# Couples' loop and the expert steps behind it: norm and routing one tanh later, Silu's table first, the softmax's exponential second

## The reference

```python
x = x + jnp.tanh(g_xattn[2]) * _L2_xattn_ref(_layernorm(x), mask, ctx, ...)
#   tanh(x@W + ctx@Ws + b) @ w over all couples (row f, text s) of a batch; softmax over s (masked);
#   tanh of the weighted sums u, v gives a scale and a shift of the normed row
x = x + jnp.tanh(g_ffn[2]) * _L2_ffn_ref(_layernorm(x), ...)
def _L2_ffn_ref(x, ...):
    weights, indices = _gate(x2, Wg)           # sigmoid, 2 of 4 groups, 4 of 16 experts
    for e in range(E):                          # E = 16, hidden 128
        we = jnp.sum(weights * (indices == e), axis=-1)
        h = jax.nn.silu(x2 @ W1[e].T + b1[e]) * (x2 @ W3[e].T + b3[e])
        y = y + (h @ W2[e].T + b2[e]) * we[:, None]
```

## Time and profile before

| | us |
|---|---|
| median of 3 runs | 599.48 (597.36 to 603.2) |
| the profiled execution | 601.89 |
| its span, first to last instruction | 600.1 |
| couples' loop, first to last sum on TensorE | 283.2 to 352.2 |
| expert steps 0 to 15 on TensorE (`up`) | 346.1 to 390.7 |

### The profile page before, as it was taken

One profiled execution on the slowest core, in us unless ns is written; L12 is line 12 of the kernel. 1 busy time (PEld: TensorE's weight loads), 2 busy tenths in 40 slices (PEclk: granted clock), 3 DMA queues, 4 the chain that ended last, 5 costly groups with the idle time before them and its releaser, 6 DMA issues.

```text
span 600.1 us, 8818 instructions
## 1 busy us (share of the span) xinstructions
PE 566.8 (94%) x3305; PEld 394.1 (66%) x3310; DVE 447.4 (75%) x696; ACT 415.2 (69%) x579; POOL 103.8 (17%) x69
## 2 busy tenths in 40 slices
PE   7999999989999999999896989999998999999997
PEld 5688787656677777775230436566545777888886
DVE  4378987588657898987989676766766847787786
ACT  4798999756755556647999765534513858888885
POOL 5400000001200000003989703200000210000000
PEclk9999999999999999999999799999998999999999
DMA  6207210200200811020000024505510110812100
GB/s 237 71 12 307 71 35 2 74 2 2 76 0 4 317 55 58 2 70 1 5 1 1 1 71 120 164 2 153 163 35 2 37 37 0 301 52 72 37 0 35
DMA packets 16782, 40.27 MB, mean 67 GB/s; under 512 B 1834, under 2 KB 6058, under 8 KB 16740
## 3 DMA queue, kind: packets, MB, share of 16 engines
q1 hardware_dynamic: 16740, 39.71, 19.9%
HBM read 39.01 MB, written 0.70 MB: 66 GB/s over the span
## 4 chain that ended last, share of the span: by engine, by line
PE 71%; DVE 14%; ACT 10%; issue 3%; POOL 1%; DVEq 0%; ACTq 0%; POOLq 0%
PE ps L713 38%; ACT work L1094 6%; PE ps L756 4%; PE ps L452 3%; DVE h_lo L1609 2%; PE ps L469 2%; PE ps L739 2%; PE ps L584 2%; PE ps L741 2%; PE ps L555 2%; PE ps L740 2%; PE ps L569 2%; PE ps L459 2%; PE ps L695 2%; DVE h_act L1586 1%
## 5 line engine op out<-in xcount | busy, mean ns | idle before, releaser
L1609 DVE TENSOR_TENSOR h_lo<-h_act,h_hi 128x512 fp32r<-128x512 f32 (+1 forms) x136 | 118.4, 874 | 39.8 <-ACT h_hi L1139 39.0
L713 PE MATMUL ps<-n_hi,w_hi 128*128 128x512 f32 (+1 forms) x232 | 85.4, 402 | 2.0 <-DVE h_act L1586 1.3
L1139 ACT CAST h_hi<-h_act 128x1024 fp32r<-128x1024 f32 (+1 forms) x88 | 75.3, 856 | 14.6 <-PE ps L713 12.1
L713 PE MATMUL ps<-n_hi,w_lo 128*128 128x512 f32 (+1 forms) x232 | 83.0, 391 | 0.0
L713 PE MATMUL ps<-n_lo,w_hi 128*128 128x512 f32 (+1 forms) x232 | 83.0, 391 | 0.0
L1817 POOL TENSOR_TENSOR rstd<-var_eps,minus_half 128x4 f32<-128x4 f32 x16 | 17.5, 1093 | 319.4 <-DVE var_eps L1273 319.4
L713 PE MATMUL ps<-h_hi,w_hi 128*128 128x512 f32 (+1 forms) x184 | 65.5, 398 | 0.1
L713 PE MATMUL ps<-h_hi,w_lo 128*128 128x512 f32 (+1 forms) x184 | 64.0, 390 | 0.0
L713 PE MATMUL ps<-h_lo,w_hi 128*128 128x512 f32 (+1 forms) x184 | 63.9, 389 | 0.0
L1094 ACT ACTIVATE work<-work,p_rest 128x2048 f32<-128x2048 f32 x31 | 59.5, 1998 | 0.4 <-DVE work L1468 0.4
L1132 ACT ACTIVATE h_act<-ps 128x512 f32<-128x512 f32 (+1 forms) x48 | 28.6, 596 | 40.4 <-PE ps L713 40.4
(11 more groups left out here) (234 smaller groups left out, 1023.7 us busy)
## 6 DMA issues: line engine op xcount, KB each, us to landing
work<-g_rows SPq DMA_DIRECT2D x36, 512.0 KB, 6.4
w_f<-in_w SPq DMA_DIRECT2D x20, 512.0 KB, 3.6
w_f<-in_w SPq DMA_DIRECT2D x8, 544.0 KB, 3.6
work<-in_w SPq DMA_DIRECT2D x2, 512.0 KB, 4.3
work<-g_rows SPq DMA_DIRECT2D x4, 256.0 KB, 9.7
p_rest<-in_p_rest SPq DMA_DIRECT2D x1, 714.0 KB, 9.8
p_attn<-in_p_attn SPq DMA_DIRECT2D x1, 546.5 KB, 6.9
x<-in_xT SPq DMA_DIRECT2D x1, 512.0 KB, 3.6
```

The costliest lines, as they stand in the source:

```text
L713: mm = pe.matmul(dst[i], wap(wt, e, lo, size, rows), mv[i], start=(first and c == 0), stop=(last and c == 2))
L1139: act.copy(places(h_hi, m, step), places(h_act, m, step)).then_inc(s["hi"], 1)
L1609: dve.tensor_tensor(lo, src, hi.bitcast(F32), ALU.subtract).then_inc(s["lo"], 1)
```

## The change

On TensorE `up(0)` and `up(1)` move one round later, ahead of the sums of rounds 30 and 31; 4 fillers stand in place of 14; steps 3 to 13 stand closer together around the bias, the weights' matmuls, the norm and the gates. On ScalarE all four first high halves come before the loop's first tanh; square and copy of norm 5 stand ahead of round 27, its high half and the first routing ahead of round 30. Behind the loop Silu's table and the Silu of steps 0 and 1 come first, then the gates' copy, the exponential's table, the softmax's exponential, and Silu's table again. `load_table` writes a column of its own each time. VectorE does products 0 and 1 ahead of the softmax, one between the halves of the weighing, and is one to three products further on at each place behind; its scratch tile `t3` is another. On GpSimd the power of norm 5, half 1, stands behind expert 10.

```diff
@@ -218,7 +218,7 @@
         pairs = work[:, 0:12 * T].rearrange("p (r c) -> p r c", r=6)
         g_all = work[:, 4 * T:12 * T].rearrange("p (e t) -> p e t", e=8)
         g_half = work[:, 4 * T:12 * T].rearrange("p (e t) -> p e t", e=16)
-        table = sb("table", [P, 1])
+        table = sb("table", [P, 16])
         h_part = [h_act[:, i // 2, (i % 2) * HALF:(i % 2 + 1) * HALF] for i in range(4)]
         h_part += [y_g[:, i // 2, (i % 2) * HALF:(i % 2 + 1) * HALF] for i in range(4)]
         values1 = vblk[0][:].rearrange("p b h c -> p (b h c)")
@@ -794,35 +794,35 @@
 
                 if L == 2:
                     for g in pair_sums():
-                        if g == 29:
+                        if g == 30:
                             pe.wait_ge(ln["lo"], 2 * L + 1)
                             up(0)
-                        if g == 30:
+                        if g == 31:
                             pe.wait_ge(x2["sumA"], own_sums(2 * B - 1))
                             up(1)
                     turn_gates((0,))
-                    keep_busy(14, 4)
+                    keep_busy(4, 4)
                     up(2)
+                    up(3)
                     out_bias(0)
-                    up(3)
+                    for step in range(4, 7):
+                        up(step)
                     weights_out(1, 0)
                     weights_out(1, 1)
-                    up(4)
+                    up(7)
                     norm_mean(5, 1)
-                    up(5)
-                    norm_var(5, 1)
-                    up(6)
-                    up(7)
-                    norm_spread(5, 1)
                     up(8)
                     up(9)
+                    norm_var(5, 1)
+                    up(10)
+                    up(11)
+                    norm_spread(5, 1)
+                    spread_gate(0)
+                    up(12)
                     logits(m, 1)
-                    up(10)
-                    spread_gate(0)
-                    up(11)
+                    for step in range(13, m.ahead):
+                        up(step)
                     spread_gate(1)
-                    for step in range(12, m.ahead):
-                        up(step)
                 elif L == 1:
                     pe.wait_ge(ln["lo"], 2 * L + 1)
                     up(0)
@@ -930,9 +930,12 @@
                     act.wait_ge(pre["txt"], 1)
                     act.copy(txt[:, half(0)], ps[:, 7]).then_inc(pre["txtcp"], 1)
 
+            loads = itertools.count()
+
             def load_table(function):
 
-                act.activation(table[:, :], minus_half[:, 0:1], function)
+                at_col = next(loads)
+                act.activation(table[:, at_col:at_col + 1], minus_half[:, 0:1], function)
 
             def copy_values(i, q):
 
@@ -1065,12 +1068,10 @@
                         ins = act.activation(dst, dst, ACT.Tanh, bias=l2b[:, 0:1])
                     ins.then_inc(x2["tanh"], 1)
 
-                for e in range(2):
+                for e in range(4):
                     first_weights(MOES[2], e)
                 copy_features(0)
                 first_tanh()
-                for e in range(2, 4):
-                    first_weights(MOES[2], e)
                 for g in range(1, 2 * B):
                     if g == 4:
                         norm_square(4, 1)
@@ -1081,10 +1082,10 @@
                         softmax_exp(0)
                     if g == 21:
                         weights_tanh(0)
-                    if g == 26:
+                    if g == 27:
                         norm_square(5, 0)
                         norm_copy(5, 0)
-                    if g == 29:
+                    if g == 30:
                         norm_high(5, 0)
                         first_routing()
                     if g in POOL_SUMS:
@@ -1159,36 +1160,37 @@
                                 split(m, e + m.slots)
 
                 if L == 2:
+                    load_table(ACT.Silu)
+                    hidden(0)
+                    hidden(1)
+                    for e in range(4, 6):
+                        split_hi_up(m, e)
                     copy_gates(0)
+                    load_table(ACT.Exp)
                     softmax_exp(1)
                     load_table(ACT.Silu)
-                    hidden(0)
-                    for e in range(4, 6):
-                        split_hi_up(m, e)
-                    hidden(1)
+                    for step in range(2, 4):
+                        hidden(step)
+                        split_hi_up(m, step + 4)
                     weights_tanh(1)
-                    for e in range(6, 8):
-                        split_hi_up(m, e)
-                    for step in range(2, 5):
+                    for step in range(4, 8):
                         hidden(step)
-                        split_hi_up(m, step + 6)
+                        split_hi_up(m, step + 4)
                     norm_square(5, 1)
                     norm_copy(5, 1)
-                    hidden(5)
-                    split_hi_up(m, 11)
-                    hidden(6)
-                    hidden(7)
-                    norm_high(5, 1)
                     hidden(8)
                     split_hi_up(m, 12)
                     hidden(9)
                     split_hi_up(m, 13)
                     hidden(10)
+                    hidden(11)
+                    norm_high(5, 1)
+                    hidden(12)
                     routing(1)
-                    for step in range(11, m.total):
+                    for step in range(13, m.total):
                         hidden(step)
-                        if step + 3 < 16:
-                            split_hi_up(m, step + 3)
+                        if step + 1 < 16:
+                            split_hi_up(m, step + 1)
                         if step == 18:
                             copy_gates(1)
                         if step in (19, 22):
@@ -1359,7 +1361,7 @@
                 update(1)
 
 
-            t3 = h_act[:, 1, 512:1024].rearrange("p (f s) -> p f s", s=S)
+            t3 = y_g[:, 1, 512:1024].rearrange("p (f s) -> p f s", s=S)
 
             def dots(t):
                 return ps[:, DOTS[t]].rearrange("p (f s) -> p f s", s=S)
@@ -1374,12 +1376,14 @@
                 link(dve.tensor_reduce(st2[:, 0], dots(t), AX, ALU.add))
                 link(dve.reciprocal(st2[:, 1], st2[:, 0]))
 
-            def weigh(t):
+            def weigh(t, between=lambda: None):
 
                 dve.wait_ge(pre["uv_in"], 128)
                 for r in range(2):
                     link(dve.tensor_tensor(t3, dots(t), bcast(uv[:, r], 1, 8), ALU.mult))
                     link(dve.tensor_reduce(stp[:, r], t3, AX, ALU.add))
+                    if r == 0:
+                        between()
                 dve.tensor_tensor(stp[:, 0:2], stp[:, 0:2], bcast(st2[:, 1], 1, 2), ALU.mult).then_inc(x2["wb"], 1)
 
             def scale_rows(t):
@@ -1659,15 +1663,18 @@
                     norm_low(5, 0)
                     for part in (route, weigh_chosen):
                         part(m, tiles=(0, HT))
+                    ahead()
+                    ahead()
                     softmax(1)
                     share(1)
-                    ahead()
-                    weigh(1)
+                    weigh(1, ahead)
                     ahead()
                     scale_rows(1)
                     ahead()
                     ahead()
+                    ahead()
                     update(1)
+                    ahead()
                     ahead()
                     ahead()
                     norm_eps(5, 1)
@@ -1676,10 +1683,9 @@
                     norm_out(5, 1)
                     ahead()
                     norm_low(5, 1)
-                    ahead()
-                    ahead()
+                    scale(0)
                     rest = lambda: None
-                    second = iter([ahead, rest, lambda: (ahead(), scale(0)), ahead, lambda: scale(1), rest, rest, rest])
+                    second = iter([ahead, rest, lambda: scale(1), rest, rest, rest, rest, rest])
                     for part in (route, weigh_chosen):
                         part(m, lambda: next(second)(), (HT, TILES))
                     for step in range(2, m.total):
@@ -1870,10 +1876,10 @@
             norm_power(4, 0)
             pair_sums()
             norm_power(5, 0)
-            for e in range(8):
+            for e in range(11):
                 low_up2(e)
             norm_power(5, 1)
-            for e in range(8, 16):
+            for e in range(11, 16):
                 low_up2(e)
             norm_power(6, 0)
             norm_power(6, 1)
```

## The result

The changed kernel is slower: 604.14 us against 599.26 (medians of 20 runs each), ratio 1.0076 with a 95% interval of 1.0057 to 1.0094. I had forecast 597.5 and a range of 593.5 to 601.3. The profiled execution has a span of 604.8 us, the kernel before 600.1. From expert step 16 on both need the same (207.4 us), so all of the difference arises ahead of it, as the prediction's yardstick supposed; only its sign is wrong.

The account below looks back on a forecast made before the run. TensorE was busy 94% of the span, with ScalarE pacing the loop; gains could arise only between about 334 and 391 us. Step 16 starting 2.0 earlier gave 599.9 from the profiled 601.89, 597.5 from the median; range 593.5 to 601.3.

Parts of the forecast that it names:

- the prediction's yardstick: Start of expert step 16 on TensorE, 392.65 us before; TensorE runs without a hole from there, so gains there last.
- TensorE meanwhile passes steps 14 and 15 without a hole: Second half, TensorE: no wait at these steps, ready for step 16 at 389.65, then waiting for product 14 until 390.65.
- 1.0 predicted: TensorE's new wait before step 11, whose low half GpSimd makes behind the norm's power: 1.0 us.
- the walk: The step-by-step timing from the loop's end to step 16, which ended in a gain of 2.0 us.
- Rival (c): A new low-clock stretch on TensorE between 356 and 376 costs 1.9 us, leaving 0.1 gain: 599.4; chance 0.08.
- that busy time no less than before holds the clock: Against a slow stretch: 11.84 busy of 15 us from 352 to 367 held clock 1.00, and no less was expected after.
- Rival (d): Second half's routing so late that step 16 waits for product 14 past 392.65: slower, 600.3 or 601.3; chance 0.10.
- page-born half: ScalarE's two added table switches each 1.4 us dearer, by the skill's page: 0.8 slower, 600.3; chance 0.05.
- The gain of 0.6: Loop's end: tanh 26 fills ScalarE's 1.95 us hole before norm 5's square; TensorE ends sum 31 0.6 us earlier, 351.65.
- TensorE's queue, not ScalarE's lead: Loop's end: ScalarE gets 2.8 us ahead, but TensorE's unbroken run of instructions gains only 0.6.
- steps 2 and 3 at 353.2: TensorE runs step 2 at 353.2, right behind four fillers, and step 3 until 356.0; they stood at 357.41 and 361.05.
- x of the second half: VectorE finishes the update at 367.5, so the second half's mean starts 1.2 us later than 366.28.

Follow-up runs that it names:

- e3: The changed kernel with nine filler matmuls on TensorE right ahead of step 14, in its wait; 601.65 us, ratio 1.0012 to the kernel before.
- e1: The changed kernel with the high halves of experts 14 and 15 made earlier, behind the Silus of steps 10 and 11; 599.85 us, ratio 0.9983.
- after: The changed kernel itself, with the whole change, against the kernel before; 604.14 us, ratio 1.0076.
- e2: e1 with the low half of expert 11 made on GpSimd ahead of the norm's power; 598.55 us, ratio 0.9973 to the kernel before.
- e9: e2 plus 5, 2, 2 and 2 filler matmuls before steps 4, 5, 6 and the second half's mean; 598.52 us, ratio 0.9957.
- e6: e2 with the loop's order as in the kernel before; 600.4 us, ratio 0.9997 to the kernel before.
- e8: The changed kernel with only the loop's part undone, experts 14 and 15 and the power still late; 604.7 us, ratio 1.0071.
- e10: e6 plus the same filler matmuls as e9; 599.2 us, ratio 0.998 to the kernel before.
- e11: The kernel before with the loop's part of the change alone, run a second time for a profile; 600.72 us, ratio 0.9998.
- e4: The kernel before with only the high halves of experts 14 and 15 moved late, behind the Silus of steps 13 and 14; 603.82 us, ratio 1.0046.
- e7: The kernel before with 4 instead of 14 filler matmuls behind the gates' transposes; 603.65 us, ratio 1.005.

## Why the prediction was wrong

*Where it failed.* The step that failed is "TensorE meanwhile passes steps 14 and 15 without a hole": a wait that I put at nothing. I had followed the power's place in GpSimd's order to step 11, and that wait came out at 1.11 us for 1.0 predicted. I did not follow the same chain, high half, low half, step, for the experts whose copies the diff moves from `step + 3` to `step + 1`. The copy of expert 14 then stands behind the Silu of step 13, which my own numbers put at 383.85 (Sigmoid done at 381.85, Silu's reload 1.3, Silu 0.7); with 0.4 for the copy and 0.7 for GpSimd, step 14 could not start before 385. My 389.65 for step 16 puts it at 382.7 (less the 6.95 that steps 14 and 15 took before, 385.70 to 392.65). The runs showed a wait of 1.98 us there, ended by GpSimd's low half, and behind it a clock at half speed. The wait was there to be read from my own numbers. Its own 1.3 us (e3 against e1) would have made 598.8 of my 597.5, inside the range; the clock behind it did the rest.

*What it cost, against the walk.* The span should have shrunk by 2.0 and grew by 4.7, 6.7 us apart. From the table: the loop began 0.64 later (two more copies of weights stand ahead of it now, but they lie in ScalarE's wait, and a matmul of the layer before, L713, is already 0.64 late, 277.74 after 277.10, so this is the execution); first sum to gates 0.24 less than predicted; gates to mean 0.27 more; mean to step 16 6.06 more. Of the last, e1 gives back 5.60: 4.3 is the clock and 1.3 the hole itself (e3). The walk without the missed wait was thus 0.5 off over 23 us.

*The clock.* Rival (c) named a stretch of low clock with a price of 1.9, placed between 356 and 376, with 0.08. It came at 386 to 395, behind the missed hole, at a price of about 4 (e3), since it lasted 9.3 us, not 3.8. That the prediction names a slow stretch at all is no credit to it: place, cause and size are others. I had taken the length of the stretch in the earlier trace rows for its usual size. The argument against it, that busy time no less than before holds the clock, came out for the changed kernel: none of after, e1, e2, e3 and e9 had a slow stretch from 356 to 376. It is no law: e6, e8 and e10, with the old loop in the changed kernel, had one, and so had e11, the kernel before with the new loop. The Trainium skill, "TensorE: Matmul & The Clock Gate", section "Part 1: The HAM clock gate", says that the gate follows how busy the engine has been recently; the trace of after agrees (1.98 us idle, then 0.63 us a matmul), and e3, where only the idle time is filled, does too. e10 shows that high busy time does not always protect.

*The tables.* Right, and cheap. ScalarE of the changed kernel in order of time:

```profile
353.29 1.28 ACT L938 ACT_TABLE_LOAD   x1
...
354.69 0.58 ACT L1049 ACTIVATE ps<-ps 128x512 f32<-128x512 f32 x1
355.29 1.28 ACT L938 ACT_TABLE_LOAD   x1
...
356.69 0.67 ACT L1133 ACTIVATE h_act<-ps,p_rest 128x512 f32<-128x512 f32 x1
```

The exponential starts at 354.69 (predicted 354.3), each load takes 1.28 us and the next activation begins at its end. Rival (d)'s page-born half, 2.66 us a switch by the Trainium skill ("ScalarE: Activation LUTs", section "What ACT_TABLE_LOAD costs"), isn't what happens here: the load at 355.29 starts 0.02 behind the exponential and Silu follows at 356.69.

*The loop.* The gain of 0.6 was the right size for this profile (0.7 from the first sum on), but for a wrong reason, so by luck. Of the 1.95 us ahead of the square, 0.32 came from the order and the rest from the slow stretch before the mean; e4, e6 and e10 show 0.32 with the same order. A hole next to a slow stretch is not a property of the order.

*Right.* TensorE's queue, not ScalarE's lead, sets the end of the loop; steps 2 and 3 at 353.2; x of the second half 1.9 later than before (1.2 predicted, and 0.64 is the later start); e1 and e2 do what the walk says, and all three runs with expert 14's half early and the new loop (e1, e2, e9) have ratios below 1, e2 and e9 clear of noise. e1, the walk without the missed wait, came out at 0.17% below the kernel before where 0.33% was forecast, and its interval holds both that and no change. Rival (d), slower, had 0.10, and its sentence "The place is product 14" was wrong: it was expert 14's weights. Above all I had no case beyond the range, because I had priced only waits that I had found.

## What to carry to other kernels

When a diff moves a helper (here a copy of weights) by a few places, follow it through all engines that stand between it and its user, each time, and put the moved thing's new finish beside its user's new start; a wait of 1.98 us on TensorE cost 5.6 here, since its clock fell behind it. If such a wait can't be avoided, a few matmuls that compute nothing, put into it, can hold the clock: e3 is 0.64% below the changed kernel by them, while in e10's profile the clock fell all the same. Before a hole in a single profile is counted as a gain, look at the granted clock around it, and if you can, at a second execution.

## What was not expected of the hardware

- The clock's slow stretches around 320 to 345 lie at different places in different executions of the same instructions, and with them the loop with the old order takes 65.7 or 68.9 us (the kernel before and e4 have the same instructions up to the gates).
- A hole of 1.98 us was followed by 9.3 us at half clock (after), one of 1.88 by some 3.5 (e4), one of 2.02 by 2.7 (e6), one of 3.81 by about 9 (e7), while one of 1.65 (before) and one of 1.28 (after) were followed by full clock; the length of the hole doesn't tell that of the stretch.
- From step 16 to the end all these kernels take either 207.4 or 205.9 us (e1, e3, e9), whatever came before. All nine profiles with 207.4 have a granted clock below 1 between 450 and 470 us (0.83 over ten microseconds, in e4 0.89 and 0.93), and none of the three with 205.9 has. The slow stretch thus goes with the 1.5 us; what decides whether it comes stays open. The ratios contain it, the columns of the table don't.
